# An attention and mixture-of-experts kernel: in the second expert loop the results are gated on ScalarE and added onto the residual rows in DRAM by the scatter

## What is computed

```
for _ in range(2):
    z_norm = rmsnorm(z, norm_w)
    scores = softmax(z_norm @ router_w)          # 8 experts
    two best experts of each token, their scores divided by their sum = gates
    mixed = sum over e of gate_e * (silu(z_norm @ w1[e]) * (z_norm @ w3[e])) @ w2[e]
    z = z + mixed
out = x + layernorm(z)
```

## Time and profile before

| | |
|---|---|
| median of 3 runs | 1092.75 us (1089.69 to 1092.95) |
| the profiled execution | 1089.77 us |
| its span, first to last instruction | 1088.0 us |
| TensorE / VectorE / ScalarE / GpSimd busy | 994.5 / 697.7 / 551.7 / 511.1 us |
| mean DMA rate | 97 GB/s |
| clock granted to TensorE, mean | 0.966 of full |

### The profile page before, as it was taken

How to read it: one execution, slowest core, us unless ns; L and a number is a source line. 1 busy time by engine, 2 the same in 40 slices (tenths; PEclk the granted TensorE clock), 3 DMA queues, 4 the chain that set the end, 5 groups by cost and what they waited for, 6 DMA issues and landing times.

```text
span 1088.0 us, 22668 instructions
## 1 busy us (share of the span) xinstructions
PE 994.5 (91%) x7114; PEld 686.5 (63%) x7114; DVE 697.7 (64%) x1635; ACT 551.7 (51%) x1075; POOL 511.1 (47%) x672
## 2 busy tenths in 40 slices
PE   4899998879999899999999999999989999999930
PEld 2578887657787767666667765667656666666620
DVE  5879988968998555784435567535596333856336
ACT  3556666648888645433334564335644333333313
POOL 2412234765787665444443354443434444554315
PEclk9989999879999999999999999999999999999975
DMA  9900000000000144323336445357344335736352
GB/s 298 369 30 0 0 0 1 1 5 25 15 19 15 30 112 118 93 77 99 88 106 166 132 117 126 89 130 176 78 120 125 88 93 131 204 105 154 82 159 92
DMA packets 137350, 105.28 MB, mean 97 GB/s; under 512 B 84528, under 2 KB 124080, under 8 KB 137264
## 3 DMA queue, kind: packets, MB, share of 16 engines
q1 hardware_dynamic: 123632, 66.88, 23.3%
q0 software_dynamic: 13632, 37.24, 11.4%
HBM read 54.27 MB, written 31.20 MB: 79 GB/s over the span
## 4 chain that ended last, share of the span: by engine, by line
PE 78%; DVE 13%; issue 3%; POOL 2%; ACT 2%; DMA 1%; SPq 0%; DVEq 0%; ACTq 0%; POOLq 0%
PE psum_s L844 32%; PE psum_o L2061 16%; PE psum_s L1571 6%; PE psum_s L2050 5%; PE psum_o L1611 5%; PE psum_t L1566 4%; PE psum_o L1606 3%; PE psum_t L690 2%; PE psum_s L1548 2%; DVE arena L1350 1%; PE psum_t L2025 1%; PE psum_y L1598 1%; DVE arena L1865 1%; DVE arena L1330 1%; DMA x_sb<-in_L_attn_x 1%
## 5 line engine op out<-in xcount | busy, mean ns | idle before, releaser
L844 PE MATMUL psum_s<-w_all,arena 128*128 x1704 | 392.0, 380 | 0.9 <-issue 0.5
L1751 POOL DMA_INDIRECT token_rows<-arena,result_row_of_row x142 | 144.8, 1020 | 308.2 <-ACT arena L1830 304.9
L844 PEld LDWEIGHTS psum_s<-w_all,arena 128*128 128x128 f16 x1704 | 158.0, 98 | 179.9 <-issue 4.7
L2061 PE MATMUL psum_o<-w_all,arena 128*128 x1704 | 209.3, 273 | 10.3 <-DVE arena L1990 10.3
L829 DVE SCALAR_TENSOR_TENSOR arena<-psum_s,gate_scale,arena 128x512 f32<-128x512 f32 x142 | 106.5, 750 | 156.0 <-PE psum_s L844 154.5
L2061 PEld LDWEIGHTS psum_o<-w_all,arena 128*128 128x128 f16 x1704 | 164.6, 98 | 54.6 <-issue 15.7
L1990 DVE TENSOR_TENSOR arena<-psum_s,arena 128x512 f16<-128x512 f32 x142 | 97.9, 690 | 130.7 <-ACT arena L1823 130.2
L1830 ACT ACTIVATE arena<-psum_o 128x256 f32<-128x256 f32 x142 | 54.4, 383 | 233.9 <-PE psum_o L2061 233.9
L805 POOL DMA_INDIRECT arena<-sorted_rows,token_of_row x142 | 142.8, 1005 | 56.6 <-issue 41.5
L823 ACT ACTIVATE arena<-psum_s,silu_scale 128x512 f32<-128x512 f32 x142 | 97.6, 687 | 102.0 <-PE psum_s L844 102.0
L1823 ACT ACTIVATE arena<-psum_s 128x512 f16<-128x512 f32 x142 | 84.7, 597 | 27.8 <-PE psum_s L2050 21.6
(11 more groups left out here) (277 smaller groups left out, 1245.1 us busy)
## 6 DMA issues: line engine op xcount, KB each, us to landing
w_all<-in_L_ffn_w SPq DMA_DIRECT2D x24, 512.0 KB, 10.3
arena<-token_rows SPq DMA_DIRECT2D x48, 256.0 KB, 3.2
sorted_rows<-w_all SPq DMA_DIRECT2D x24, 256.0 KB, 2.3
out<-x_sb SPq DMA_DIRECT2D x8, 512.0 KB, 3.0
arena<-token_rows SPq DMA_DIRECT2D x8, 512.0 KB, 7.6
arena<-sorted_rows,token_of_row POOLq DMA_INDIRECT x142
arena<-arena SPq DMA_TRANSPOSE x142
token_rows<-arena,result_row_of_row POOLq DMA_INDIRECT x142, 2.4
```

Source lines behind the costliest of these rows:

```text
L844: last = nc.tensor.matmul(bank, e_xT[:, u, lx * DC + c, :], w_split[:, bass.ds(e * EW + at, FF)], start=(q == 0), stop=(q == 3 * DC - 1))
L1751: nc.gpsimd.indirect_dma_start(rows, bass.IndirectOffsetOnAxis(ap=targets[:, at : at + 1], axis=0), y_row[:, u, :], None).then_inc(s_sent[ ...
L2061: last = nc.tensor.matmul(psum_e, hT[:, lh, c, :], w_split[:, bass.ds(e * EW + at, D)], start=(q == 0), stop=(q == 3 * FC - 1))
```

## The change

In the second loop the residual rows live in DRAM while the experts run. Passes 1 and 2 store each combined pair of token tiles of z to `z_rows` (`store_z`, 8 stores of 256 KB for each half), and 896 KB more are stored once for the empty slots' rows (`store_spare`). The gates are stored to a DRAM table when they are known (`store_gates`), and `fetch` issues a second gather for each tile of passes 2 and 3, one 4-byte gate for each row, by a list `gate_index` that the index step computes with six more linked instructions (`gate_places`). `y_copy` multiplies by that gate (`scale=`). `send` no longer writes a place of its own for each choice but adds onto the token's row of `z_rows`. Since both results of a token go to one row, a scatter waits until the one before it has landed. In pass 3 `load_z` loads 8 x 256 KB of finished z where `load_half` loaded 16 x 256 KB and VectorE added; the tail loads 4 x 512 KB and has no gated additions, and VectorE adds two of every group's four tiles to x, GpSimd two.

```diff
+        z_rows = expert_rows[0]
+        gate_words = 2 * B * S
+        gate_table = expert_rows[1].rearrange("r (d o) -> (r d) o", o=1)[0:gate_words, :]
+        gate_view = gate_table.rearrange("(p c h t) o -> p h c (t o)", c=2, h=B, t=NT)
...
+        def gate_places(link, at, second, result):
+
+            row = sources[:, at]
+            place = place_int[:, 0 : at.stop - at.start]
+            link(nc.vector.tensor_scalar(place, row, P - 1, 6, ALU.bitwise_and, ALU.logical_shift_left))
+            link(nc.vector.tensor_copy(result, place))
+            link(nc.vector.tensor_scalar(place, row, 7, None, ALU.logical_shift_right))
+            link(nc.vector.scalar_tensor_tensor(second, second, 1.0 / (2 * S // P * 2), result, ALU.mult, ALU.add))
+            link(nc.vector.tensor_copy(result, place))
+            link(nc.vector.tensor_tensor(gate_index[at.start > 0], second, result, ALU.add))
...
+                link(nc.vector.tensor_scalar(sources[:, 0:FULL], above, -1.0, 0.0, ALU.add, ALU.max))
+                if r:
+                    gate_places(link, slice(0, FULL), second, result)
+                    nc.vector.tensor_scalar(targets[:, 0:FULL], above, -1.0, None, ALU.add).then_inc(s_index, 1)
+                else:
+                    nc.vector.scalar_tensor_tensor(targets[:, 0:FULL], above, -1.0, second, ALU.add, ALU.add).then_inc(s_index, 1)
...
-                nc.vector.tensor_tensor(second, second, late, ALU.add)
                 link(nc.vector.tensor_tensor(above, above, late, ALU.add))
-                nc.vector.tensor_scalar(sources[:, FULL:COLUMNS], above, -1.0, 0.0, ALU.add, ALU.max)
-                link(nc.vector.scalar_tensor_tensor(row, above, -1.0, second, ALU.add, ALU.add))
-                nc.vector.tensor_tensor(targets[:, FULL:COLUMNS], row, none, ALU.max).then_inc(s_index, 1)
+                link(nc.vector.tensor_scalar(sources[:, FULL:COLUMNS], above, -1.0, 0.0, ALU.add, ALU.max))
+                if r < B:
+                    link(nc.vector.tensor_tensor(second, second, late, ALU.add))
+                    link(nc.vector.scalar_tensor_tensor(row, above, -1.0, second, ALU.add, ALU.add))
+                    nc.vector.tensor_tensor(targets[:, FULL:COLUMNS], row, none, ALU.max).then_inc(s_index, 1)
+                else:
+                    gate_places(link, slice(FULL, COLUMNS), second, row)
+                    link(nc.vector.tensor_scalar(none, none, -1.0 * B * S, None, ALU.add))
+                    nc.vector.scalar_tensor_tensor(targets[:, FULL:COLUMNS], above, -1.0, none, ALU.add, ALU.max).then_inc(s_index, 1)
...
+                if k >= B:
+                    pool.wait_ge(s_gate_st[k % B], 16 * (2 if k == B else 4))
...
+            if k >= B:
+                nc.gpsimd.indirect_dma_start(
+                    gate_row[:, at : at + 1], None, gate_table,
+                    bass.IndirectOffsetOnAxis(ap=gate_index[k % B][:, t : t + 1], axis=0)).then_inc(s_fetch[u], 16)
...
+            def store_z(k, p):
+
+                h = (k - 1) % B
+                sp.wait_ge(s_z, (B + k - 1) * NT + 2 * p + 2)
+                at = h * S + 2 * p * P
+                sp.dma_start(z_rows[at : at + 2 * P, :].rearrange("(g p) d -> p g d", p=P),
+                             z_tile(h * NT + 2 * p, 0, 2 * D).rearrange("p (g d) -> p g d", d=D)).then_inc(s_z_st[h], 16)
+
+            def store_spare():
+
+                sp.dma_start(z_rows[B * S :, :].rearrange("(g p) d -> p g d", p=P), x_rows[:, 0 : NE - 1, :]).then_inc(s_spare, 16)
+
+            def store_gates(k):
+
+                h = (k + 1) % B
+                sp.wait_ge(s_gates, k + 1)
+                for c in range(2):
+                    sp.dma_start(gate_view[:, h, c, :], gates[:, h, c, :]).then_inc(s_gate_st[h], 16)
+
+            def load_z(p):
+
+                at = 2 * p * P
+                sp.dma_start(z_tile(2 * p, 0, 2 * D).rearrange("p (g d) -> p g d", d=D),
+                             z_rows[at : at + 2 * P, :].rearrange("(g p) d -> p g d", p=P)).then_inc(s_z_back[p // 2], 16)
...
-                        for p in range(2):
+                        for p in range(2 if k < END else 0):
                             load_half(k, p)
-                    if k and 2 <= t - plan.combine + 1 < PAIRS:
+                    if k in (1, 2) and 2 <= t - plan.combine + 1 < PAIRS:
                         load_half(k, t - plan.combine + 1)
+                    if k in (1, 2) and 0 <= t - plan.combine - 1 < PAIRS:
+                        store_z(k, t - plan.combine - 1)
+                    if k == END and 0 <= t - plan.load < PAIRS:
+                        load_z(t - plan.load)
+                    if k < END and t == plan.gates + 1:
+                        store_gates(k)
+                    if k == 2 and t == 0:
+                        store_spare()
                     if k < END and 0 <= t - plan.split - 1 < PAIRS:
                         store_rows(k, t - plan.split - 1)
...
-            sp.wait_ge(s_z, (B + END) * NT)
-            sp.wait_ge(s_out_r, NT)
             for q in range(QUADS):
-                for c in range(2):
-                    at = (2 * order[END][1] + c) * S + q * slots * P
-                    sp.dma_start(last_results[q][:, :, c, :],
-                                 token_rows[at : at + slots * P, :].rearrange("(g p) d -> p g d", p=P)).then_inc(s_tok[q], 16)
+                at = S + q * slots * P
+                sp.dma_start(z_tile(NT + q * slots, 0, slots * D).rearrange("p (g d) -> p g d", d=D),
+                             z_rows[at : at + slots * P, :].rearrange("(g p) d -> p g d", p=P)).then_inc(s_tok[q], 16)
...
                 pool.wait_ge(s_yrow, n + 1)
-                if k % B == 0:
-                    rows = token_rows[0 : 2 * S, :]
-                else:
-                    rows = token_rows[:, :]
-                nc.gpsimd.indirect_dma_start(
-                    rows, bass.IndirectOffsetOnAxis(ap=targets[:, at : at + 1], axis=0),
-                    y_row[:, u, :], None).then_inc(s_sent[u], 16)
+                where = bass.IndirectOffsetOnAxis(ap=targets[:, at : at + 1], axis=0)
+                if k < B:
+                    nc.gpsimd.indirect_dma_start(token_rows[0 : 2 * S, :] if k == 0 else token_rows[:, :], where,
+                                                 y_row[:, u, :], None).then_inc(s_sent[u], 16)
+                    return
+                if t == 0:
+                    pool.wait_ge(s_z_st[k % B], 16 * PAIRS)
+                    if k == END:
+                        pool.wait_ge(s_spare, 16)
+                if n > FIRST[B]:
+                    pool.wait_ge(s_sent[(n - 1) % UNROLL], 16 * ((n - 1) // UNROLL + 1))
+                nc.gpsimd.indirect_dma_start(z_rows[0:S, :] if k % B == 0 else z_rows[:, :], where, y_row[:, u, :], None,
+                                             compute_op=ALU.add).then_inc(s_sent[u], 16)
...
-                for g in range(slots if q < QUADS - 1 else slots // 2):
+                for g in range(slots // 2):
...
-                nc.scalar.activation(y_row[:, u, :], psum_e, ACT.Copy).then_inc(s_yrow, 1)
+                if k < B:
+                    nc.scalar.activation(y_row[:, u, :], psum_e, ACT.Copy).then_inc(s_yrow, 1)
+                else:
+                    nc.scalar.activation(y_row[:, u, :], psum_e, ACT.Copy, scale=gate_row[:, at : at + 1]).then_inc(s_yrow, 1)
...
-                    combine(END - 1, p)
-                    final_stats(END - 1, (2 * p, 2 * p + 1))
+                    dve.wait_ge(s_z_back[p // 2], 16 * 2)
+                    final_stats(0, (2 * p, 2 * p + 1))
...
+            def last_sums(q):
+
+                for g in range(slots // 2, slots):
+                    j = NT + q * slots + g
+                    dve.wait_ge(s_out_t, j + 1)
+                    nc.vector.tensor_tensor(x_sb[:, tile_of(j)], x_sb[:, tile_of(j)], z_tile(j), ALU.add).then_inc(s_out_v, 1)
+
             for q in range(QUADS):
-                tiles = tuple(range(q * slots, (q + 1) * slots))
-                dve.wait_ge(s_tok[q], 32)
-                add_results(END, last_results[q], tiles)
-                final_stats(END, tiles)
+                dve.wait_ge(s_tok[q], 16)
+                final_stats(1, tuple(range(q * slots, (q + 1) * slots)))
                 dve.wait_ge(s_fstat, (B + 1) * NT + (q + 1) * slots)
                 variance(link, 1, slice(q * slots, (q + 1) * slots), -0.5)
-            for j in range(2 * NT - slots // 2, 2 * NT):
-                dve.wait_ge(s_out_t, j + 1)
-                nc.vector.tensor_tensor(x_sb[:, tile_of(j)], x_sb[:, tile_of(j)], z_tile(j), ALU.add).then_inc(s_out_r, 1)
+                if q:
+                    last_sums(q - 1)
+            last_sums(QUADS - 1)
```

36 lines of the change are left out of this document (24 added, 12 removed).

## The result

The changed kernel takes 1122.05 us (median of 4, 1119.38 to 1132.13), the kernel before 1092.2 in the runs beside it: ratio 1.029, 95% interval 1.023 to 1.036. It is 2.9% slower where 1.1% faster was forecast, and lies above the range.

The account below looks back on a forecast made before the run. TensorE bounds the loop and VectorE paces the tail. Tail -12.4, last landing +0.9, index step +0.4, stores +0.5 give -10.6 us: 1079.2 from 1089.77, or 1082.2 with the runs' offset; forecast 1081, range 1074 to 1100.

Parts of the forecast that it names:

- The tail: After the last scatter: first load -1.5, work 29.04 to 18.1 us, last store the same; -12.4 us, landing +0.9.
- the late engine: In the tail's work GpSimd, no longer VectorE, would be late next, with a turn of 3.8 us per group.
- The whole sum outside the scatter and the gather: Tail -12.4, index step +0.4 and stores +0.5 us, without the adding scatter's +0.9.
- The index step: Before pass 3, linked VectorE instructions make it 1.5 us longer; TensorE waits 0.4 us.
- The stores of z: 16 stores of 256 KB in SyncE's queue; 0.5 us allowed together with the 896 KB and the gate stores.
- I take L = 2.4 + 0.9 = 3.3, nearest to those rows: Adding scatter's time from issue to landing: plain scatter's 2.4 us plus 0.9 for a read leg.
- The prediction's estimate from this: Alternative landing time of the adding scatter: doubling the 1.45 us behind the instruction gives 3.9 us, costing +2.0 instead of +0.9.
- It costs nothing while L is under the beat of 4.36 us: Second loop: waiting for the previous scatter's landing is free, as scatters start 4.36 us apart; 1.05 us of cover.
- rival A: Chain of scatters sets the beat if issue to landing exceeds 4.36 us; 1103 us at 4.8; chance 0.13.
- free if the adding scatter takes no more than 1.8 us to issue: GpSimd's added gate gather takes 1.28 of 2.09 us idle per beat, leaving 0.8, so it costs nothing.
- Rival B: GpSimd becomes the bound if the adding scatter's instruction takes 1.95 us, turn 4.8; about 1100 us; chance 0.06.
- matters to nobody: Transpose gather on GpSimd, issued four tiles ahead, comes 1.3 us later because of the added gate gather, at no cost.

Follow-up runs that it names:

- e5: Changed kernel without gate gather (constant scale), with plain writes to own places instead of adds and no wait between scatters: 1079.0 us, ratio 0.989.
- e17: Second timing of the changed kernel without gate gather, adds or wait between scatters: 1079.7 us, ratio 0.990.
- e3: Changed kernel without the second gather of each tile, ScalarE scaling by a constant; adds and their chain stay: 1110.9 us, ratio 1.015.
- e1_no_chain: Changed kernel with each second-loop scatter adding onto a place of its own, so none waits for the one before: 1110.6 us, ratio 1.016.
- e14: Second timing of the changed kernel with plain writes to own places, no chain, gate gather issued but unread: 1122.7 us, ratio 1.030.
- e4: Changed kernel with plain writes to own places instead of adds, no chain; gates still gathered and applied: 1130.1 us, ratio 1.036.
- e9: Changed kernel with plain writes to own places, no chain, gate gather issued but ScalarE scaling by a constant: 1076.6 us, ratio 0.990.

## Why the prediction was wrong, point by point

**The tail: right, with a little luck.** Forecast -12.4 before the add's own landing, which was to give back 0.9: -11.5. Measured: first load 5.61 to 4.05 (-1.56 for -1.5), work 29.04 to 18.12 (-10.92 for -10.9), store -0.92 for 0, landing +1.26 for +0.9; together -12.1. The work is right, but GpSimd did not become the late engine as was said: the roots of groups 2 and 3 still waited for VectorE (0.44 and 0.45 us), and GpSimd is busy 10.92 of the 18.12 us, VectorE 15.07. The whole sum outside the scatter and the gather was -12.4 + 0.4 + 0.5 = -11.5, and e5 and e17 stand 10.2 (B) and 12.4 (A) below the kernel before. The index step came as forecast: in the changed kernel's trace `h_lo` starts at 843.05, 2.18 us after L646 (840.87), where it was 0.73, so +1.45 for +1.5; TensorE waited 0.23 us behind it for 0.4. The stores of z were not measured by themselves. ScalarE's copy with the scale takes 0.47 us and not 0.38, which the prediction put at nothing; e5 and e17 have it too and lose nothing by it.

**The adding scatter's landing: a term taken too small.** The step "I take L = 2.4 + 0.9 = 3.3, nearest to those rows" failed. L is 3.9 to 4.0 at the median. The 0.9 for the read leg was right: the 1.45 us behind the instruction became 3.9 - 1.59 = 2.3. What was left out is GpSimd's own part of L: the instruction takes 1.59 us and not 0.98, 0.6 more, which the prediction put at nothing in L. By the Trainium skill, page "Collectives: The Full Stack", section "The bandwidth ceiling: the fold count and why AG ≠ RS ≠ AR", the add of a ring's reduction needs two source reads in place of one and so halves the rate. The prediction's estimate from this was 3.9 in all. The traces agree with that sum by chance only: the 1.45 us became 2.3 and not 2.9, and the 0.6 of GpSimd made up for it.

**"It costs nothing while L is under the beat of 4.36 us": the step that failed and decided it.** A link of the chain is not L but L and the time from the landing to the next start, 0.77 us, which I left out. The threshold for L was 4.36 - 0.77 = 3.6, and not 4.36. So even with the landing of 4.0, which by my rule had 0.36 us to spare, the chain sets the beat. This is rival A, at 0.13, though not by its own condition, L over 4.36, which the median never met; its price is nearly right (22 at L = 4.8; a link of 4.8 is what came, and the slow landings add the rest to 38). In the changed kernel itself adds and chain without the gather cost 31 us (e3 against e17), and the gather on top of them 11. I had also taken L as one number; its tail, up to 6.6 us, costs in a chain and is free elsewhere.

**GpSimd: a gap forgotten.** The step "free if the adding scatter takes no more than 1.8 us to issue" was wrong by the 0.30 us that stand before every indirect instruction. 2.09 us of idle time hold only 1.79 that can be filled. The timeline of GpSimd in e1_no_chain, at place A, shows the full queue:

```profile
956.58 1.63 POOL L1836 DMA_INDIRECT token_rows<-arena,result_row_of_row  x1 [0.30 <-issue]
958.51 0.99 POOL L847 DMA_INDIRECT arena<-sorted_rows,token_of_row  x1 [0.30 <-issue]
959.80 0.95 POOL L851 DMA_INDIRECT arena<-expert_rows,amax_g  x1 [0.30 <-issue]
961.06 1.62 POOL L1836 DMA_INDIRECT token_rows<-arena,result_row_of_row  x1 [0.31 <-issue]
```

From scatter to scatter 961.06 - 956.58 = 4.48 us with nothing awaited: 1.62 + 0.99 + 0.95 and three gaps of 0.30. That is 0.12 over the beat, some 6 us for 50 tiles by my estimate, and no slack behind any delay. Rival B held in this small size, at a scatter of 1.62 us and not of 1.95. e1 loses 31 us against e17, and no run here parts the full queue from the gather's loss at A: gather and adds together without the chain were not timed at B.

**The gate gather: "matters to nobody".** At B that is right: 1076.6 with it, 1079.0 without. At A it costs 43 to 50 us, and the changed kernel was profiled at A. The kernel before has no such gather and was profiled at B, so its profile could not show this. The two losses don't add: e17 1079.7, with add and chain 1110.9, with the gather as well 1122.05, all at A. Perhaps a beat that one of them has stretched leaves room for the other; that is argued and not shown.

**What stays open.** Why VectorE and ScalarE start late behind TensorE at place A, in gaps 25 to 32 us apart; whether recording the execution takes part in it, since place A is known mainly by a trace with completions missing; whether the gather needs the rest of the change for it; and why plain writes with the gather (1122.7 to 1130.1) are slower than adds with it (e1, 1110.6). What the changed kernel takes at B wasn't measured.

## What to carry to other kernels

When a queue waits for its own last transfer, the link of that chain is issue, landing and restart together, and it is to be compared with the beat with its slow cases in it, not with its median; here a chain of two cost nothing where a chain of one cost 38 us. When an instruction is added to a full queue, count its gap with it. And when the same kernel gives two times, look for something in an unchanged part that tells the places apart before explaining the difference by the change: four runs of it agreed each time and misled me for one theory. And before a landing time is read from a trace, count its completions: with some of the 16 missing, the last one recorded comes too early.

## What was not expected of the hardware

An adding scatter of 128 rows of 1 KB takes GpSimd 1.59 us in place of 0.98 and lands in 3.9 to 4.0 us in place of 2.4, up to 6.6 to 7.5. From a landing to the start of the scatter that waits for it are 0.77 us. A 4-byte gather for each tile cost 43 us or more in the changed kernel with plain writes at place A (e14, e4) and nothing at place B (e9).
